# Layer 1's attention with its row maxima folded into the queries, and a new order of its steps

## What is computed

```python
x = x + pos_emb
w = x.reshape(B, nW, 64, H, hd)                      # windows of 64, 16 heads of 8
attn = softmax(einsum('bnqhd,bnkhd->bnhqk', w, w) * scale)
local = einsum('bnhqk,bnkhd->bnqhd', attn, w)
comp = conv1d(x, conv_w, stride=4)[:, :64] + conv_b  # 64 compressed keys
gt = concat([comp, global_memory])                   # and 64 fixed ones
ga = softmax(einsum('bshd,bghd->bhsg', x, gt) * scale)
glob = einsum('bhsg,bghd->bshd', ga, gt)
mix = sigmoid(concat([local, glob]) @ gate_w + gate_b)
out = (mix * local + (1 - mix) * glob) @ out_w + out_b
```

## Time and profile before

| | us |
|---|---|
| median of 3 runs | 1380.31 (1378.35 to 1384.34) |
| the profiled execution | 1372.89 |
| its span | 1371.1 |
| starts of `again_global(i, 0)`, i = 0 to 3 | 577.46, 637.81, 689.29, 741.03 |
| i = 4 to 7 | 792.47, 843.99, 897.19, 948.40 |

### The profile page before, as it was taken

How to read it: one execution, slowest core, us unless ns; L and a number is a source line. 1 busy time by engine, 2 the same in 40 slices (tenths; PEclk the granted TensorE clock), 3 DMA queues, 4 the chain that set the end, 5 groups by cost and what they waited for, 6 DMA issues and landing times.

```text
span 1371.1 us, 20897 instructions
## 1 busy us (share of the span) xinstructions
PE 1123.0 (82%) x6836; PEld 670.0 (49%) x6836; DVE 800.4 (58%) x2040; ACT 502.0 (37%) x1137; POOL 583.9 (43%) x708
## 2 busy tenths in 40 slices
PE   2778787876649994699999999999942899999990
PEld 1356554555325663345556556456531455555550
DVE  2488888987422223435647767756554455565565
ACT  1334444433315553032442443343410344434440
POOL 0257777777524554503234455452353123222321
PEclk9999999998679997579999999999955999999995
DMA  7676776563145222101101112001112511111106
GB/s 295 146 184 158 171 180 151 131 167 86 39 117 192 79 78 71 59 9 36 37 26 48 31 49 63 27 28 30 29 43 69 173 32 35 36 37 35 36 20 192
DMA packets 96047, 117.28 MB, mean 86 GB/s; under 512 B 11176, under 2 KB 81320, under 8 KB 92984
## 3 DMA queue, kind: packets, MB, share of 16 engines
q1 hardware_dynamic: 86984, 97.46, 26.7%
q0 software_dynamic: 8704, 17.97, 4.0%
q10 hardware_dynamic: 256, 0.53, 0.2%
HBM read 85.35 MB, written 32.17 MB: 86 GB/s over the span
## 4 chain that ended last, share of the span: by engine, by line
PE 49%; DVE 5%; issue 3%; POOL 1%; DMA 1%; SPq 1%; ACT 1%; POOLq 0%; DVEq 0%; ACTq 0%
PE bank L1976 9%; PE bank L2218 4%; PE bank L1962 4%; PE bank L2161 4%; PE bank L2115 3%; PE bank L1986 3%; PE bank L2168 3%; PE bank L2198 2%; PE bank L2127 2%; PE bank L1970 2%; PE bank L2200 2%; PE bank L2187 2%; PE bank L2232 1%; PE bank L2183 1%; PE bank L1746 1%
## 5 line engine op out<-in xcount | busy, mean ns | idle before, releaser
L1163 POOL DMA_INDIRECT slots<-pay,slot x128 | 129.4, 1011 | 82.5 <-issue 71.6
L1178 POOL DMA_INDIRECT y<-region,xin x80 | 76.8, 960 | 190.9 <-ACT region L1540 170.6
L1976 PE MATMUL bank<-wgl,rows 128*128 x288 | 138.5, 604 | 5.8 <-ACT rows L1523 5.8
L979 DVE TENSOR_REDUCE rows<-bank 128x4 f32<-128x512 f32 x128 | 79.4, 683 | 74.4 <-PE bank L2115 74.1
L1523 ACT ACTIVATE rows<-bank 128x256 f32<-128x256 f32 x216 | 80.8, 382 | 101.4 <-PE bank L1970 100.3
L1178 POOL DMA_INDIRECT y<-hh,region x64 | 61.2, 957 | 119.9 <-ACT hh L1540 105.3
L734 DVE TENSOR_TENSOR rows<-bank,w0uv 128x512 f32<-128x512 f32 x72 | 49.7, 691 | 95.5 <-PE bank L1976 86.8
L1659 ACT ACTIVATE w0uv<-bank 128x512 f32<-128x512 f32 x128 | 66.1, 603 | 88.7 <-PE bank L2168 88.7
L726 DVE TENSOR_TENSOR rows<-region,bank 128x256 f32<-128x256 f32 x72 | 30.3, 421 | 113.4 <-ACT region L1528 113.4
L1970 PEld LDWEIGHTS bank<-consts,rows 128*128 128x128 f32 x432 | 57.9, 142 | 73.8 <-issue 50.6
L1201 POOL TENSOR_TENSOR region<-region 128x512 f32<-128x512 f32 x64 | 81.4, 1285 | 13.9 <-DVE region L866 12.8
(11 more groups left out here) (320 smaller groups left out, 2412.1 us busy)
## 6 DMA issues: line engine op xcount, KB each, us to landing
region<-vrdram SPq DMA_DIRECT2D x16, 1024.0 KB, 9.4
region<-vrdram SPq DMA_DIRECT2D x32, 512.0 KB, 8.7
xin<-slots SPq DMA_DIRECT2D x80, 65.0 KB
region<-slots SPq DMA_DIRECT2D x64, 65.0 KB
wgl<-in_wgl SPq DMA_DIRECT2D x1, 4096.0 KB, 13.0
rows<-y SPq DMA_DIRECT2D x8, 512.0 KB, 4.3
wgl<-y SPq DMA_DIRECT2D x8, 512.0 KB, 7.5
xres<-x SPq DMA_DIRECT2D x12, 256.0 KB, 2.3
```

The source lines that it names most:

```text
L979: V.tensor_reduce(maxg[:, t, g * QD:g * QD + HG], bank[g].rearrange("p (h k) -> p h k", h=HG), axis=AX, op=ALU.max).then_inc(S["c_mx"], 1)
L1163: p.indirect_dma_start(io["slots"], bass.IndirectOffsetOnAxis(ap=slot_of(l, b)[:, k, t:t + 1], axis=0), pay_of(l, b)[:, k, t, :], None).th ...
L1178: p.indirect_dma_start(io["y"], bass.IndirectOffsetOnAxis(ap=xins[par][:, h, k, P + 1:P + 2].bitcast(U32), axis=0), bYs[par][:, h, k, :], ...
L1976: ins = M(bank[k][:, :], bT[:, k, tile(c)], wgl[:, bass.ds(ex_of[h][k], 1), c, :].squeeze(1), start=c == 0, stop=c == FC - 1)
```

## The change

- The negated maximum is no longer added by a matmul. A new `queries(b)` on DVE multiplies the turned maxima (bank 7) by a vector that is -1 in one row of each head's eight channels and 0 elsewhere, and adds the masked queries `xmk`, into `xneg` (four times 128 x 512, in the room of `b12`). The row used is one of another head, which the mask has zeroed. `keys_again(b)` on ACT writes `gmk1`, the masked keys with a 1 in that row. `again_global` then is one matmul per bank, of `gmk1` and `xneg`. `less_global`, `less_max_global`, `negmax` and `pick_g` go.
- `max_T_global(a)` moves from the step of row i into the end of the step before, and `queries(a)` to the end of DVE's step.
- Two local units, `attend_local(b, 1, 0)` and `(b, 1, 1)`, stand in the head of the next step, with their `norm_local`; the first stood at the end of the own step. `UNIT_BANK` becomes ((6, 4), (7, 6)), and `attend_local(b, 1, 0)` waits for all of `queries(b + 1)`, which read bank 7.
- The order of the steps on PE, DVE and ACT is new. On DVE `norm_global(i)` comes after `max_global(a, 2)`, `modulate` before it; `add_front` and `stats_front` come after `queries` where there is no row i yet.
- `gmk` has one buffer in place of two. `b12` is loaded by SP in its tail, after the last `c_E`.

```diff
         mgb = wa0[:, NT, :]
-        gmk = [rows[:, 9 + i, :].rearrange("p (r k) -> p r k", r=HG) for i in range(2)]
-        negmax = rows[:, 11, :]
+        gmk, gmk1 = (rows[:, 9 + i, :].rearrange("p (r k) -> p r k", r=HG) for i in range(2))
+        xneg = b12[:, 0:4, :]
...
         UNITS = SG + SL
-        UNIT_BANK = ((6, 7), (4, 6))
-        S_STEPS, E_STEPS, PV_STEPS, REC_STEPS, NEG_STEPS, VA_STEPS = 32, 32, 8, 5, 5, 5
-        MASKS = 30
+        UNIT_BANK = ((6, 4), (7, 6))
+        S_STEPS, E_STEPS, PV_STEPS, REC_STEPS, NEG_STEPS, VA_STEPS = 32, 32, 8, 5, 2 * HG, 5
...
+                sp.wait_ge(S["c_E"], NB * E_STEPS)
+                settled(sp)
+                sp.dma_start(b12[:, :, :], io["b12"].partition_broadcast(P)).then_inc(S["load_b"], 16)
...
 
             def max_global(b, t):
 
...
-                    V.tensor_reduce(maxg[:, t, g * QD:g * QD + HG], bank[g].rearrange("p (h k) -> p h k", h=HG),
+                    V.tensor_reduce(maxg[:, t, heads(g)].rearrange("p (r x) -> p r x", x=DH)[:, :, 0], bank[g].rearrange("p (h k) -> p h k", h=HG),
                                     axis=AX, op=ALU.max).then_inc(S["c_mx"], 1)
+
+            def queries(b):
+
+                v.wait_ge(S["c_max_t"], 2 * b + 1)
+                v.wait_ge(S["c_xm"], b * HG + HG)
+                if b:
+                    v.wait_ge(S["c_E"], (b - 1) * E_STEPS + NHG * HG)
+                for r in range(HG):
+                    V.scalar_tensor_tensor(out=xneg[:, r, :], in0=bank[7], scalar=negrow[:, HG - 1 - r:HG - r], in1=xmk[b % 2][:, r, :],
+                                           op0=ALU.mult, op1=ALU.add).then_inc(S["c_neg"], 1)
 
             def max_local(b, l):
 
...
                 a, b, c, d, f = i + 1, i - 1, i - 2, i - 3, i + 2
+                if ok(b):
+                    norm_local(b, 1, 0)
+                    norm_local(b, 1, 1)
                 if ok(i):
                     max_local(i, 0)
-                if ok(b):
-                    norm_local(b, 1, 1)
-                if ok(a):
-                    global_keys(a, a % 2)
+                if ok(a):
+                    global_keys(a)
                 if ok(d):
                     router(1, d, 0.0, 0)
                 if ok(i):
                     place(1, d)
                 if ok(a):
                     max_global(a, 0)
-                if ok(f):
+                if ok(f) and ok(i):
                     add_front(f)
                     stats_front(f)
                 if ok(a):
                     max_global(a, 1)
                 if ok(b):
                     mix(b, b % 2)
-                if ok(i):
-                    norm_global(i, i % 2)
-                if ok(a):
-                    max_global(a, 2)
                 if ok(c):
                     modulate(c)
+                if ok(a):
+                    max_global(a, 2)
+                if ok(i):
+                    norm_global(i, i % 2)
                 if ok(b):
                     residual(b)
                 if ok(i):
                     max_global(a, 3)
                 if ok(i):
                     norm_local(i, 0, 1)
-                    norm_local(i, 1, 0)
+                if ok(a):
+                    queries(a)
+                if ok(f) and not ok(i):
+                    add_front(f)
+                    stats_front(f)
                 if ok(f):
                     positions(f, f % 2)
 
             def tail(t):
+                norm_local(t, 1, 0)
                 norm_local(t, 1, 1)
                 modulate(t - 1)
...
 
-            def less_max_global(b):
-                a.wait_ge(S["c_max_t"], 2 * b + 1)
-                A.activation(negmax, bank[7], ACT.Copy, scale=-1.0).then_inc(S["c_neg"], 1)
+            def keys_again(b):
+                a.wait_ge(S["c_gm"], 2 * b + 1)
+                for r in range(HG):
+                    ins = A.activation(gmk1[:, r, :], gtT[:, :], ACT.Identity, scale=mask4[:, r:r + 1],
+                                       bias=mask32[:, DH * (HG - 1 - r):DH * (HG - 1 - r) + 1])
+                ins.then_inc(S["c_gm"], 1)
 
             def less_max_local(b):
...
                 a, b, c, d, f = i + 1, i - 1, i - 2, i - 3, i + 2
-                if ok(i):
-                    less_max_global(i)
                 if ok(b):
                     mixed_T(b, b % 2, 0)
                 if ok(i):
                     exps(i, 0)
                 if ok(a):
                     compressed(a)
+                if ok(i):
+                    exps(i, 1)
                 if ok(d):
                     second_copy(1, d)
-                if ok(i):
-                    exps(i, 1)
-                if ok(d):
                     second_exp(d)
                 if ok(b):
                     mixed_T(b, b % 2, 1)
                 if ok(i):
                     exps(i, 2)
                     less_max_local(i)
+                    exps(i, 3)
                     local_values(i)
-                    exps(i, 3)
+                if ok(a):
+                    keys_again(a)
                 if ok(b):
                     gate_tanh(b)
...
-                    t_.wait_ge(S["c_nl"], normed(b - 1, 0, 1))
+                    t_.wait_ge(S["c_ng"], b)
                 for t in range(NT):
                     ins = nc.tensor.transpose(bank[7][:, tile(t)], maxg[:, t, :], ident)
                 ins.then_inc(S["c_max_t"], 1)
...
                 else:
                     t_.wait_ge(S["c_exp"], b * UNITS + (k - 1) * NHG + g + 1)
 
-            def again_global(b, p, r):
-
+            def again_global(b, r):
+
+                t_.wait_ge(S["c_gm"], 2 * b + 2)
+                t_.wait_ge(S["c_neg"], b * NEG_STEPS + r + 1)
                 for g in range(NHG):
                     bank_free(b, r, g)
-                    M(bank[g], gmk[p][heads(g), r, :], xTs[p][heads(g), :], start=True, stop=False)
-
-            def less_global(b, r):
-
-                if r == 0:
-                    t_.wait_ge(S["c_neg"], b * NEG_STEPS + 1)
-                for g in range(NHG):
-                    M(bank[g], pick_g[heads(g), r, :], negmax[heads(g), :], start=False, stop=True).then_inc(S["c_E"], 1)
+                    M(bank[g], gmk1[heads(g), r, :], xneg[heads(g), r, :], start=True, stop=True).then_inc(S["c_E"], 1)
 
             def again_local(b, p, l):
 
...
                     t_.wait_ge(S["c_va"], b * VA_STEPS + 1)
-                    t_.wait_ge(S["c_neg"], b * NEG_STEPS + 1)
+                    t_.wait_ge(S["c_neg"], b * NEG_STEPS + HG)
...
                     t_.wait_ge(S["c_ng"], b + 1)
+                    if t and b:
+                        t_.wait_ge(S["c_x"], b)
                 elif t == 0:
-                    if b:
-                        t_.wait_ge(S["c_x"], b)
-                    else:
-                        t_.wait_ge(S["c_va"], VA_STEPS)
+                    if b + 1 < NB:
+                        t_.wait_ge(S["c_neg"], (b + 1) * NEG_STEPS + HG)
                 else:
                     t_.wait_ge(S["c_nl"], normed(b, 0, 0))
...
                 a, b, c, d, f, p = i + 1, i - 1, i - 2, i - 3, i + 2, i % 2
-                if ok(i):
-                    again_global(i, p, 0)
-                    max_T_global(i)
                 if ok(b):
                     turn_out(b, 0)
-                if ok(i):
-                    less_global(i, 0)
+                if ok(b):
+                    attend_local(b, 1, 0)
+                if ok(i):
+                    again_global(i, 0)
+                if ok(b):
+                    attend_local(b, 1, 1)
+                if ok(i):
+                    score_local(i, p, 0)
+                    again_global(i, 1)
                 if ok(a):
                     compress(a, a % 2)
                 if ok(i):
-                    score_local(i, p, 0)
-                if ok(b):
-                    attend_local(b, 1, 1)
+                    attend_global(i, 0)
                 if ok(d):
                     route(d)
                 if ok(i):
-                    again_global(i, p, 1)
-                    less_global(i, 1)
-                    attend_global(i, 0)
                     score_local(i, p, 1)
                 if ok(b):
                     turn_out(b, 1)
+                if ok(i):
+                    attend_global(i, 1)
                 if ok(d):
                     rank(1, d)
                 if ok(i):
-                    again_global(i, p, 2)
-                    less_global(i, 2)
-                    attend_global(i, 1)
+                    again_global(i, 2)
+                if ok(a):
+                    score_global(a, a % 2, 0)
+                if ok(i):
                     max_T_local(i)
-                if ok(a):
-                    score_global(a, a % 2, 0)
-                if ok(i):
+                    again_global(i, 3)
                     attend_global(i, 2)
                     local_values(i, p)
-                    again_global(i, p, 3)
-                    less_global(i, 3)
```

(17 more changed lines are left out.)

32 lines of the change are left out of this document (18 added, 14 removed).

## The result

| | before | after |
|---|---|---|
| median of 4 runs, us | 1379.33 (1374.00 to 1384.34) | 1546.84 (1546.33 to 1551.18) |
| span of the profiled execution | 1371.1 | 1545.1 |
| granted clock over the span | 0.901 | 0.808 |

The ratio is 1.122 (95% interval 1.1175 to 1.1269): 167 us slower. The forecast was 1458, the range ended at 1500. Direction and mechanism came out, the size did not.

A forecast was written before the change was run, and what follows sets the result against it. PE was taken to bound the kernel, with about an eighth to spare. Full-clock terms of +55 and +24 for the clock gave +79 on the profiled 1372.9, 1452, and 1458 us with most of the median's excess; own range 1435 to 1480, 8-in-10 1405 to 1500.

The forecast's parts named there:

- What is removed: less_global's matmuls leave PE in each attention step: 4.3 us a step, 34 us over eight if nothing else changed.
- The waits of the walk: Attention step followed at full clock: 18.9 us of stalls, longest 6.75 before attend_local(i, 0, 0); 59.8 us against 51.4.
- The start: Start of the attention stage: add_front(1) and statistics behind queries(0) delay the first exponentials to about 593.5, +8.5 us.
- The clock: Attention steps: new waits lower PE's clock to 0.78 in every step; 4 us in each of six, +24, bounds 0 and +48.
- Step 0: First attention step, with no row b behind it, 60.4 us long before: +0 to +4 us, 2 taken.
- Step 7 and tail: End of the attention stage: no scores of a next row, so no long stall; tail gains two units; -1 us.
- (1): Whole kernel: PE's relief from less_global decides, the new waits cost nothing; 1355 us, chance 0.05.
- (2): Attention steps: relief and waits cancel, only the 5.3 us wait lasts; +11, up to 1392 us, chance 0.06.
- (3): Attention steps: only half of the new short waits lasts beside the long one, no clock loss; 1422 us, chance 0.19.
- (4): Attention steps: PE's clock low through most of each step, +8 to +12 a step; 1495 us, chance 0.18.
- Theory C: Attention steps: waits are as walked; the excess is PE's low clock in and behind them, some 15 us of 75.

The follow-up runs named there:

- the pairs that add only work: Unneeded matmuls in PE's waits: kernel before with late norm_global, +67.2 to +45.6; changed kernel with old orders restored, +34.1 to -7.7; changed kernel, four places, +158.0 to +62.5.
- Norm: Changed kernel with norm_global(i) back ahead of max_global(a, 2): 1517.07 us, +96.3. Kernel before with norm_global(i) moved late, alone: 1487.94 us, +67.2.
- head covers: Changed kernel with compress before score_local(i, 0), and attend_local(b, 1, 1) and route before again_global(i, 1), as before the change: 1544.36 us, +137.6.
- front: Changed kernel with add_front and stats_front back between max_global(a, 0) and (a, 1) where there is no row i: 1554.69 us, +142.7.
- middle: Changed kernel with PE's order from attend_global(i, 1) to score_global(a, 2) as before the change: 1563.76 us, +151.8.
- the three filling matmuls: Changed kernel with four orders restored, plus unneeded matmuls: two ahead of max_T_global, one ahead of attend_local(b, 1, 0): 1409.86 us, -7.7; without them 1446.10, +34.1.

## Why the prediction was wrong, by its own steps

**Right.** *What is removed*: 34 us "if nothing else changed"; with the order kept the change gives 30. `queries` "2.8 to 3.3 us": 2.73. The late `b12` load: "nothing", and the 346 us behind the stage are equal to 0.1. `keys_again`, in ScalarE's idle time: 1.65 us, nothing waits for it. *The waits of the walk*: `max_T_global` 1.99 (2.3 said), `turn_out` 0.96 (1.0), `norm_global` 6.51 (6.75), each with its releaser. The waits for banks show as idle time only in part (1.13 ahead of `again_global(i, 1)`, 0.78 ahead of `score_global(a, 0)`); the rest lies inside the groups. The stalls that the walk names add up to 17.6, where its sum has 18.9. *The start*: "exponentials start about 593.5", they start at 592.1, 7.0 later than before (8.5 said).

**The step that failed is the one called "The clock".** It gave 4 us a step, at most 8. The walk at full clock beside the step that was measured (us from the start of `again_local(i, 1)` to the start of the named group; measured from 864.09):

| group | walk | measured | excess in the stretch up to it |
|---|---|---|---|
| `max_T_global(a)` | 8.6 | 9.8 | 1.2 |
| `again_global(0)` | 14.1 | 17.6 | 2.3 |
| `compress` | 21.9 | 30.0 | 4.6 |
| `again_global(2)` | 30.4 | 40.4 | 1.9 |
| `max_T_local` | 35.5 | 46.0 | 0.5 |
| `attend_global(2)` | 38.7 | 50.7 | 1.5 |
| `score_global(a, 2)` | 49.9 | 63.8 | 1.9 |
| `attend_local(i, 0, 0)` | 57.95 | 71.75 | -0.1 |
| the next `again_local(i, 1)` | 59.8 | 75.3 | 1.7 |

The excess is 15.5 us, and it lies where PE works at the low level, not where it waits: the stretch with the long wait has none. The two stretches from `max_T_global` to `compress` hold 6.9 of it, at a clock of 0.52:

```profile
873.90:894.10 20.20, 18.11 (x96) 12.94 (x96) 8.17 (x18) 3.60 (x7) 7.78 (x7) 0.52 0.00 1
```

Three things were wrong in the term. The list of what lengthens left out the local units: three of them at 3.6 us instead of 1.9 make 5.1, the largest share, in the stretches with 2.3, 4.6 and 1.7. It ended with `attend_global(0)`, while `attend_global(2)` too took 3.6 us (914.80 to 918.37) and `again_global(3)` 3.7. And it took step 0's clock, 0.78, for every step, while the step had 0.70, with 11.4 us of idle PE in 75.3 against 3.1 in step 0's 50. The forecast had the mechanism, and its rows, but sized it by a list of groups instead of by all that PE does.

Two other terms fell short. Step 0 was not walked: +2 said, +10.0 measured, and that is not the clock but waits, for PE is idle 13.6 us of it where it was idle 3.8, with the same wait of 6.4 us for `norm_global` as in the steps behind it and 2.6 for the maxima. Step 7 and tail: -1 said, +15.9 measured. There PE is busy 12.5 us longer, at a clock of 0.63 against 0.84, which is the failed step again; it also has a wait of 3.35 us for `norm_global`, where the text said that no scores of a next row are there and so no long stall. The start was forecast by the first exponentials and came out, `front_T(1)` and its wait of 11.3 us for GpSimd's norm included. Counted by `again_global(0, 0)` it is +12.4, and what this has more than 8.5 belongs to step 0 if both are counted from the exponentials (+7.0 and +15.5). With steps 1 to 6 (69.2 said with the clock, 135.7 measured) the shortfalls are 8.0 + 16.9 + 3.9 + 66.5 = 95.3, which but for rounding is the difference between 174.0 and 79.

**The rivals.** (1), (2) and (3) would have needed waits shorter than walked; no stretch of the table is clearly shorter than the walk. (4) had the right mechanism, "low through most of each step", and was priced at 8 to 12 us a step; measured was 15. Its 1495 stood inside the range, but the range stopped 5 us above it and so held no room for its own error. Theory C is borne out in its cause by the pairs that add only work: their seven steps are 24, 35 and 66 us shorter (22, 42 and 95 by the whole times), and the clock rises each time. In its sizes it missed with several kernels. The Trainium skill, "TensorE: Matmul & The Clock Gate", "Why this matters for your kernels", advises against idle gaps of the tensor engine between bursts of matmuls. This case agrees: the seven steps take 517 to 523 us with the gaps and 451 with unneeded matmuls in them.

**What stays open.** The parts of the order don't add up to its whole. Norm (-62 of 158 when undone, +67 alone), head covers (-20), front (-15 by the whole time, -10 by its stretch), middle (-6): together -103, while undoing all four gives -124, and the rest, +34 above before, goes with three filling matmuls. By the seven steps, without the scatter of the kernel before, the gap is wider: norm -40, covers -19, front +1, middle -2, together -59 (the front's 10 us lie ahead of the steps), and all four -102. That the parts share one clock, so that what one is worth depends on the others, fits this but was not shown. The kernel with the three filling matmuls lies below the kernel before only by the execution beside it; its seven steps, 386.5, are longer than the 370.9 and 382.2 of the kernel before. What makes VectorE and ScalarE start late is open too.

## What to carry to other kernels

On engines that run in order, follow for each moved instruction who waits for what stands behind it, and price a wait of PE twice: its length, and the groups around it at the low clock, all of them, narrow ones and weight loads included. Make a change of arithmetic in the old order first, measure it, and only then reorder. If a wait of PE can't be covered by useful work, a few matmuls into a free bank are a cheap trial of what the clock takes.

## What the runs showed of the hardware that was not expected

- At the low clock a 128 x 128 weight load takes 333 ns for 192, and a matmul of only 34 columns goes from a median of 278 to 406; the group of 16 from 1.9 to 3.6 us. Narrow work is not spared.
- Short waits are enough here to leave the clock low: with 3.4 us of idle PE in a step of 58, most of it the waits at its head, 1.99 and 0.96 us in the step shown, the clock was 0.79; with three matmuls more in those waits it was 0.97. Idle time alone doesn't tell the clock: a later step of that kernel has 4.6 us of it and 0.91.
- The kernel before has steps (1 to 6) of 51.2 to 53.2 us in one execution and 51.4 to 56.9 in another, where the four longer than 51.4 have a late start, and took 1404 to 1421 us in single executions on other chips, where its median beside the change was 1379.
- VectorE's maxima or ScalarE's exponentials and copies start 1.5 to 4 us later than usual in some steps of most of the kernels timed once, and in none of the first profiles of the two kernels, with nothing in the trace that names the cause.
